# The experts' gate product moves from ScalarE and GpSimd to VectorE

## The reference

```
h = jnp.einsum('bsd,edf->bsef', x, W1)
g = jnp.einsum('bsd,edf->bsef', x, W3) + b3
act = jax.nn.silu(h) * g
out = jnp.einsum('bse,bsef,efd->bsd', C, act, W2)
```

## Time and profile before

| what | value |
|---|---|
| time, median of 3 runs | 3892.0 us (3887.76 to 3893.32) |
| the profiled execution's own time | 3894.85 us |
| its span, first to last instruction | 3893.0 us |
| mean granted clock of TensorE | 0.906 of full speed |
| busy over the span | TensorE 82%, VectorE 77%, GpSimd 75%, ScalarE 62% |
| first scan to last scan | 90.7 us to 3408.3 us |

### The profile page before, as it was taken

How to read it: one execution, slowest core, us unless ns; L and a number is a source line. 1 busy time by engine, 2 the same in 40 slices (tenths; PEclk the granted TensorE clock), 3 DMA queues, 4 the chain that set the end, 5 groups by cost and what they waited for, 6 DMA issues and landing times.

```text
span 3893.0 us, 68598 instructions
## 1 busy us (share of the span) xinstructions
PE 3175.9 (82%) x17390; PEld 2022.7 (52%) x17390; DVE 2985.2 (77%) x5234; ACT 2417.3 (62%) x5390; POOL 2913.4 (75%) x3055
## 2 busy tenths in 40 slices
PE   5687888778889888988889888988889888777782
PEld 3233354335556555655556555655556555556672
DVE  2698989988898888888888888888898888822110
ACT  2454576456757766676756767676757767665451
POOL 1465667685769897888968897888968887976755
PEclk8788898789989998999989999999989998987996
DMA  3965656465869677886869677886869677856783
GB/s 83 221 148 136 151 131 163 121 160 138 223 172 256 162 206 197 229 216 160 232 178 249 167 203 201 229 218 161 228 186 252 165 196 204 234 157 181 236 243 109
DMA packets 420320, 730.00 MB, mean 188 GB/s; under 512 B 56203, under 2 KB 313814, under 8 KB 417750
## 3 DMA queue, kind: packets, MB, share of 16 engines
q1 hardware_dynamic: 302422, 484.13, 49.9%
q10 hardware_dynamic: 99072, 203.47, 17.1%
q0 software_dynamic: 18432, 37.93, 3.6%
HBM read 596.93 MB, written 100.07 MB: 179 GB/s over the span
## 4 chain that ended last, share of the span: by engine, by line
PE 25%; POOL 23%; issue 21%; DVE 15%; ACT 9%; DMA 3%; ACTq 2%; SPq 1%; POOLq 1%; DVEq 0%; PEldq 0%
POOL prod L698 11%; DVE state L1584 6%; PE ps_conv L901 6%; PE ps_main L967 5%; DVE ps_x L1571 3%; PE ps_g L1085 2%; POOL got L821 2%; POOL rows_in L798 2%; POOL hidden L810 2%; PE ps_g L1092 2%; PE ps_y L981 2%; PE ps_h L1073 2%; PE ps_x L915 2%; DMA dt_rep<-dt_dram 1%; ACT g_sb L1392 1%
## 5 line engine op out<-in xcount | busy, mean ns | idle before, releaser
L698 POOL TENSOR_TENSOR prod<-state,c_rep 128x384 f32<-128x384 f32 x1536 | 1534.4, 1008 | 587.3 <-DVE state L1584 569.3
L1584 DVE TENSOR_TENSOR_SCAN state<-dt_rep,carry,ps_x 128x384 f32<-128x384 f32 x1280 | 1285.1, 1004 | 0.0
L1571 DVE TENSOR_TENSOR ps_x<-ps_x,db_rep 128x384 f32<-128x384 f32 x1536 | 852.7, 555 | 243.0 <-PE ps_x L915 230.3
L1208 ACT ACTIVATE dt_rep<-dt_rep,vecs 128x768 f32<-128x768 f32 x768 | 718.3, 936 | 144.0 <-DMA dt_rep<-dt_dram 100.0
L915 PE MATMUL ps_x<-x_stack,copy 96*128 96x384 bf16 x1536 | 534.9, 350 | 304.1 <-DVE state L1584 300.7
L901 PE MATMUL ps_conv<-gx,w_conv 128*128 128x384 f32 x1728 | 690.6, 507 | 7.8 <-DVE parts L1601 4.6
L915 PEld LDWEIGHTS ps_x<-x_stack,copy 96*128 96x128 bf16 x1536 | 154.0, 100 | 680.5 <-DVE state L1584 491.4
L1392 ACT ACTIVATE g_sb<-ps_g,w_down 128x128 f32<-128x128 f32 x1032 | 305.0, 371 | 263.6 <-PE ps_g L1092 257.1
L901 PEld LDWEIGHTS ps_conv<-gx,w_conv 128*128 128x128 f32 x1728 | 302.1, 195 | 218.6 <-issue 131.8
L1073 PE MATMUL ps_h<-u_t,w_up 128*128 128x128 f32 x2064 | 329.0, 299 | 101.4 <-DVE silu L1801 77.8
L810 POOL TENSOR_TENSOR hidden<-g_sb,silu 128x384 f32<-128x384 f32 x344 | 344.4, 1001 | 81.2 <-ACT u_out L1398 72.1
(11 more groups left out here) (256 smaller groups left out, 4960.1 us busy)
## 6 DMA issues: line engine op xcount, KB each, us to landing
dt_rep<-dt_dram SPq DMA_DIRECT2D x384, 768.0 KB
w_up<-in_w_exp ACTq DMA_DIRECT2D x344, 384.0 KB, 5.1
w_down<-in_w_exp ACTq DMA_DIRECT2D x344, 193.5 KB
x_stack<-parts SPq DMA_DIRECT2D x576, 48.0 KB
u_in<-rows_in SPq DMA_DIRECT2D x344, 64.5 KB
rows_out<-u_out SPq DMA_DIRECT2D x344, 64.0 KB
dt_dram<-dt SPq DMA_DIRECT2D x192, 96.0 KB
qv<-in_x SPq DMA_DIRECT2D x48, 192.0 KB
```

What stands on the lines that cost most here:

```text
L698: pool.tensor_tensor(prod[:, k % HS, :], state[:, k % HS, :], c_rep[:, c % 2, :], ALU.mult).then_inc(s_prod.sem, 1)
L1208: act.activation(dt_rep[:, g % XS, q:q + 2, :], dt_rep[:, g % XS, q:q + 2, :], ACT.Exp, scale=decay_rate).then_inc(s_decay.sem, 2)
L1571: dve.tensor_tensor(x_n, x_n, db_rep[:, c % 2, :], ALU.mult).then_inc(s_inflow.sem, 1)
L1584: dve.tensor_tensor_scan(state[:, k % HS, :], dt_rep[:, g % XS, q, :], ps_x[k % XB][:, 0:T], init, ALU.mult, ALU.add).then_inc(s_state.sem, 1)
```

## The change

ScalarE no longer moves `g` to SBUF, and GpSimd no longer multiplies. Instead VectorE, directly behind its L1801, forms `hidden = (g + bias) * silu` straight from `ps_g`, in three instructions of 128x128 (one for each column of the bias). VectorE now waits there for its own L1801 to have finished, for `ps_g` to be full and for the bias to have landed. ScalarE, before it reads the result of the tile two before from the same bank, waits until VectorE is done with it; `ps_g` is freed by `u_out` as before. The buffer `g_sb` goes.

```diff
-        hidden, silu, g_sb = sb("hidden", [P, HID, F]), sb("silu", [P, 2, F]), sb("g_sb", [P, 2, F])
+        hidden, silu = sb("hidden", [P, HID, F]), sb("silu", [P, 2, F])
...
             def experts(m, t):
                 if m is None:
                     return
-                u = tile_of.get(t - 3)
-                if u is not None and u < NU:
-                    pool.wait_ge(*read(m, f"h{u}"))
-                    pool.wait_ge(*read(m, f"g{u}"))
-                    if u >= HID:
-                        pool.wait_ge(*full(m, f"g{u - HID + LAG}"))
-                    pool.tensor_tensor(hidden[:, u % HID, :], g_sb[:, u % 2, :], silu[:, u % 2, :], ALU.mult).then_inc(s_hidden.sem, 1)
...
                 act.wait_ge(*full(m, name))
                 if u < NU:
-                    due(act, s_down[u % WB], m, u // WB + 1)
-                    for k in range(MF):
-                        o = slice(P * k, P * k + P)
-                        ins = act.activation(g_sb[:, u % 2, o], aux(name)[:, o], ACT.Identity,
-                                             bias=w_down[:, u % WB, F + k:F + k + 1])
+                    due(act, s_hidden, m, u + 1)
                 v = u - LAG
                 if v >= 0:
                     if v >= UOUT:
                         due(act, s_ostore[v % UOUT], m, v // UOUT)
-                    ins = act.activation(u_out[:, v % UOUT, :], aux(name)[:, F:F + P], ACT.Copy, scale=u_in[:, v % UIN, D:D + 1])
-                ins.then_inc(frees(name), 1)
+                    act.activation(u_out[:, v % UOUT, :], aux(name)[:, F:F + P], ACT.Copy, scale=u_in[:, v % UIN, D:D + 1]).then_inc(frees(name), 1)
+                else:
+                    act.sem_inc(frees(name), 1)
...
                     dve.scalar_tensor_tensor(out=silu[:, u % 2, :], in0=silu[:, u % 2, :], scalar=1.0, in1=aux(f"h{u}")[:, 0:F],
                                              op0=ALU.add, op1=ALU.mult).then_inc(frees(f"h{u}"), 1)
+                    dve.wait_ge(*read(m, f"h{u}"))
+                    dve.wait_ge(*full(m, f"g{u}"))
+                    due(dve, s_down[u % WB], m, u // WB + 1)
+                    for k in range(MF):
+                        o = slice(P * k, P * k + P)
+                        ins = dve.scalar_tensor_tensor(out=hidden[:, u % HID, o], in0=aux(f"g{u}")[:, o],
+                                                       scalar=w_down[:, u % WB, F + k:F + k + 1], in1=silu[:, u % 2, o],
+                                                       op0=ALU.add, op1=ALU.mult)
+                    ins.then_inc(s_hidden.sem, 1)
```

## The result

The changed kernel takes 4188.65 us (median of 4 runs, 4188.3 to 4196.61) against 3889.88 for the kernel before in the same sessions: a ratio of 1.0773, with an interval of 1.0757 to 1.0789. The forecast of slower holds; the size does not: +299 us where +88 stood, and 119 us above the upper end of the range.

The account below looks back on a forecast made before the run. VectorE was taken to bind in passes without tiles, VectorE and TensorE by turns with tiles. Terms 88 + 8 + 7 - 5 - 10 = +88 on 3894.85 gave 3983, 3980 us against the median; 8-in-10 range 3910 to 4070.

Parts of the forecast that it names:

- What ScalarE's new wait does: ScalarE's queue: `u_out` 1.5 us later, mostly taken up by its idle time; +8 us, bounds 0 and 60.
- The tail, +7: Behind the last scan: the bank's chain takes 1.33 us in place of 1.20, 53 tiles; +7 us, 0 to +15.
- The price of the products: VectorE behind L1801: three instructions 0.81 us plus 0.12 wait, 0.93 a tile; bounds 0.77 and 1.10.
- The wait for `ps_g`: VectorE ahead of the products, between the scans: `g` is full before L1801 ends, so 0.
- The cover: Between the scans: each stretch's idle covers its own tile's 0.93; the rest, 15.3 us a pass, gives +88 us.
- GpSimd's relief, -10 of at most 31: Whole span: waits for GpSimd's L810, at most 31 us, partly go; a third taken, 10 us off.
- No cover at all: Between the scans: every tile pays 0.93 us whole, 231 us, with a lower clock; about 4120; chance 0.14.
- Pooled cover: Between the scans: stretches lend each other idle through three `ps_x` banks, +20 us; 3904, or 3946 at 1.10; chance 0.18.
- Faster, because GpSimd is relieved: VectorE's idle, pooled over a pass, covers all products; all 31 us of waits for L810 go; 3861; chance 0.06.
- the one set for this failure: Forecast wrong if VectorE's waits for ScalarE's copies or tanh grow by over 40 us.
- its wait for the spread: VectorE's waits for TensorE's spread, 230.3 us before, were to be roughly halved.
- 92%: VectorE was to be busy 92% or more between first tile and last scan.

Follow-up runs that it names:

- Issue ahead of the wait: The change, with ScalarE issuing the weights' loads before it waits for VectorE's products, not behind `u_out`; 4016.46 us, 1.0317 to before.
- `u_out` first: The change, but ScalarE moves the result out once `ps_g` is full; VectorE's products follow and free the bank; 3948.97 us, 1.0150 to before.
- The load alone: Kernel before, plus three instructions of the products' form, results unused, on VectorE behind each L1801 between the scans; 3952.12 us, 1.0152.
- The half loads: Kernel before, plus three unused-result instructions on VectorE behind 21 tiles a pass with 1.0 us idle or more, or the other 22; 3906.71 and 3953.16 us.
- The load where idle: Kernel before, plus three unused-result instructions on VectorE behind only the 21 tiles a pass with 1.0 us idle or more; 3906.71 us, 1.0028.
- the real products on these tiles: Kernel before, with products on VectorE and `u_out` ahead of them for only the 21 tiles a pass where VectorE was idle; 3880.88 us, 0.9966.

## Why the prediction was right or wrong

**The failed step is "What ScalarE's new wait does", +8 with 60 as the upper bound.** The prediction named everything queued behind `u_out`, and then took a shift of 1.5 us as mostly taken up because ScalarE was busy only 196.30 of 277.64 us. The runs put 232 - 61 = 171 us on it between the scans, by subtraction of the load's cost. A mean share of busy time says nothing here. What is queued behind `u_out` is what VectorE and TensorE need next: from first to last scan VectorE waits 185 us for ScalarE, 104 before. And between the two stands the loads' issue, during which ScalarE has no work. Issue ahead of the wait gives back 157 of the 232. The issue's length alone is not the cost: with `u_out` first ScalarE stands behind it just as long, and the scans lose no more than the load's +61 to +63. It costs where ScalarE is already late, behind the wait for VectorE. Later weights are not the way it costs, since in the trace of the change TensorE waits 1.0 us in all for them. How much of the 157 is the issue's own time there, and how much the length of the queue that it holds, no run separates.

The Trainium skill ("Perfetto Trace Analysis", sections "DVE / Act Engine Instruction" and "DMA Instruction — HWDGE") has this difference: an instruction for the engine is pushed into a queue and the sequencer goes on to the next, while a DMA's issue keeps the sequencer until it is done. Both traces agree: before, the first issue, at 3602.65, runs beside work already queued; after, `u_t` waits 1.50 us behind it.

**The tail, +7, fails by the same step.** Its chain began at L1801, taken as ready when `ps_g` is full, though the row has it wait 2.28 us for ScalarE's tanh. After the change the tanh for it stands behind the previous `u_out` and the issue, so the loop is 3.83 and not 2.97: 0.97 x 53 tiles is 51 of the +61 us.

**The price of the products was a little low.** Three take 0.87 us (forecast 0.81), 345 ns each, a little above the 0.24 to 0.33 that was to be seen; the gap to L1791 is 0.19 to 0.21 in most tiles of the passes and 0.04 in the others (forecast 0.12), 0.15 on the mean. That is 1.02 in all, against 0.93 and bounds of 0.77 and 1.10. The last overlaps the next multiplication by 0.09, which saves nothing, as L1801 of the earlier trace rows did so before. The rows of that overlap, before and after:

```profile
2483.94 0.56 DVE L1571 TENSOR_TENSOR ps_x<-ps_x,db_rep 128x384 f32<-128x384 f32 x1
```

```profile
2657.25 0.56 DVE L1561 TENSOR_TENSOR ps_x<-ps_x,db_rep 128x384 f32<-128x384 f32 x1
```

The wait for `ps_g` is 0.6 us in all between the scans, put at 0.

**The cover was right in its direction and too small in size.** The load alone cost +61, the products with `u_out` first +63, where 88 was forecast. The gap is larger than it looks: by the prediction's own sum the load's 0.90 a tile comes to 84 us (15.3 less 23 x 0.03 a pass) and the products' 1.02 to some 100. VectorE's busy time rises from first to last scan by 3068.69 - 2877.85 = 190.8 us for 248 tiles, 0.77 each; at 0.77 the sum gives 67, but 0.77 is not the time that a tile's products take. The half loads confirm that place decides; what covered the rest stays open. The price, 0.09 too low for the products, hid 12 us of that.

**GpSimd's relief, -10 of at most 31, is not measured apart.** The load where idle costs +12 us, and with the real products on these tiles the kernel gains 13. So some 25 us come from what ScalarE and GpSimd no longer do, for half the tiles, ScalarE's three evacuations included. That is more than was put; the tanh's wait for GpSimd's product fell by 21.7.

**The rivals.** "No cover at all" is nearest in time, 4120, and wrong in its mechanism: a good part of the load is covered. "Pooled cover" is refuted by the half loads, as idle of a whole pass would cover either half. "Faster, because GpSimd is relieved" fails for the whole change, and holds for the tiles where VectorE has room, with `u_out` first. The rule from the Trainium skill ("GPSIMD Engine Reference", section "Engine selection") is right on which engine is faster, three in 0.87 us against 1.0, though not by half here. It says nothing of the hand-over, which decided. Of the signs, the one set for this failure came: VectorE's waits for ScalarE's `y_sq`, `parts` and `ps_main` grew by some 60 us together; its wait for the spread fell by 71 and not by half; 92% was not reached. The three waits in the kernel before:

```profile
DVE sz L1621 <- ACT y_sq L1301: 15.2, 10, 5.1
DVE parts L1601 <- ACT parts L1255: 4.6, 10, 1.4
DVE y L1646 <- ACT ps_main L1320: 14.5, 18, 2.8
```

## What to carry to other kernels

When an instruction gets a new wait, follow its queue on to the next instruction that another engine needs, and price what stands between, the issue of transfers too: here it was cheap ahead of the wait or without one, and dear behind it. If two engines read one buffer, let the one with the longer queue behind it go first. Idle time covers new work mostly in the stretch where it lies, so move work tile by tile to where there is room: with `u_out` first, the 21 tiles of a pass where VectorE had room made the kernel 0.3% faster, all 43 made it 1.5% slower.

## What the runs showed of the hardware

- Issuing two loads whose address is read from memory keeps ScalarE without work for 1.27 to 1.50 us in the rows shown where nothing else is queued on it, though each issue's own row shows 0.34 to 0.37. Beside the evacuations, in the row of the tail before, it was 0.44.
- Moving these issues to SyncE cost 1.3% by itself, since the rows' loads then stood behind them, as above. The Trainium skill ("DMA: Bandwidth & Descriptors", section "Issuing engines are not separate DMA queues") says that another issuing engine saves only the sequencer's time, which is usually small relative to the transfer. What that time is worth hangs on what waits for it: between the scans the kernel before gained nothing by the move, and the change 232 - 78 = 154 us.
- The granted clock was lower where TensorE stood more: in the passes with tiles TensorE is idle 502 us in the change and 357 before, at 0.92 and 0.93. From first to last scan it is 0.90 in the change and 0.92 before, so more of the time is at 1.2 in place of 2.4 GHz, and the same matmuls take longer:

```profile
91.00:3640.00 3549.00, 2889.27 (x15136) 1743.16 (x15136) 3068.69 (x5702) 1961.10 (x3893) 2359.04 (x2445) 0.90 0.69 178
```

```profile
91.00:3408.00 3317.00, 2809.77 (x15130) 1719.27 (x15129) 2877.85 (x4956) 2154.83 (x4637) 2584.74 (x2689) 0.92 0.73 191
```

TensorE's busy time is 79 us longer for nearly the same count. With the loads issued ahead of the wait the clock is 0.94 with tiles, with the same work on every engine, so it was not the work moved to VectorE that lowered it. Whether the slower matmuls are a part of the change's loss is not shown; VectorE's waits for the spread did not grow with them.
